# Causal attention on one core: value products of two steps issued in one run

## The reference

```python
Q = (X @ Wq.T + bq).reshape(B, S, H, d_head) * scale
K = (X @ Wk.T + bk).reshape(B, S, H, d_head) * scale
V = (X @ Wv.T + bv).reshape(B, S, H, d_head)
scores = jnp.einsum('bqhd,bkhd->bhqk', Q, K)
causal = jnp.tril(jnp.ones((S, S), bool))
scores = jnp.where(causal[None, None], scores, -jnp.inf)
attn = jax.nn.softmax(scores.astype(jnp.float32), axis=-1).astype(X.dtype)
out = jnp.einsum('bhqk,bkhd->bqhd', attn, V).reshape(B, S, D)
return out @ Wo.T + bo
```

## Time and profile before

| | |
|---|---|
| median of 3 runs | 2092.39 us (2077.45 to 2098.33) |
| profiled execution, span | 2086.8 us |
| TensorE busy | 1742.4 us (83%) |
| VectorE busy | 1398.7 us (67%) |
| ScalarE busy | 966.8 us (46%) |
| scores L1817, 768 | 304.2 us busy |
| units L1796, 768 | 254.2 us busy |
| values L1829, 1536 | 162.7 us busy |
| exponentials L1780, 768 | 346.4 us busy |
| row maxima L1697, 608 | 372.1 us busy |

### The profile page before, as it was taken

The page is one execution under the profiler, slowest core; times in us unless marked ns, Lnnn a source line. Parts: engine busy times, 40 slices in busy tenths (PEclk is TensorE's granted clock), DMA queues, the critical chain, the costliest instruction groups (busy, mean ns, idle before and its releaser), DMA issues. The chain is left out here.

```text
span 2086.8 us, 35358 instructions
## 1 busy us (share of the span) xinstructions
PE 1742.4 (83%) x10488; PEld 1335.8 (64%) x10488; DVE 1398.7 (67%) x2854; ACT 966.8 (46%) x2226; POOL 677.7 (32%) x845
## 2 busy tenths in 40 slices
PE   6998897189964664999999899996899999758886
PEld 5887785179963452554554454444699999647775
DVE  5567998056657865999777676643666776436666
ACT  2454564044435650565655555564434444323333
POOL 2444588300017612112146456520000000355540
PEclk8678999599986986999999999999999999879998
DMA  9213356344435874424245344315844444534441
GB/s 344 72 46 76 92 136 173 126 143 125 125 109 169 283 264 93 97 56 94 63 117 143 101 136 137 105 53 150 245 153 126 125 124 127 164 89 137 145 130 34
DMA packets 291880, 272.78 MB, mean 131 GB/s; under 512 B 138153, under 2 KB 260714, under 8 KB 289644
## 3 DMA queue, kind: packets, MB, share of 16 engines
q1 hardware_dynamic: 267960, 215.41, 35.6%
q0 software_dynamic: 18432, 50.36, 7.8%
q10 hardware_dynamic: 5332, 4.96, 0.7%
HBM read 136.84 MB, written 133.69 MB: 130 GB/s over the span
## 5 line engine op out<-in xcount | busy, mean ns | idle before, releaser
L1780 ACT ACTIVATE ca_PT<-ca_psS 128x512 f32<-128x512 f32 (+3 forms) x768 | 346.4, 492 | 285.5 <-PE ca_psS L1817 243.3
L1697 DVE TENSOR_REDUCE ca_part<-ca_psM 128x1 f32<-128x512 f32 (+3 forms) x608 | 372.1, 657 | 137.9 <-PE ca_psM L1800 104.6
L1817 PE MATMUL ca_psS<-ca_QS,ca_KS 128*128 128x512 f32 (+3 forms) x768 | 304.2, 403 | 12.3 <-ACT ca_PT L1780 12.1
L1796 PE MATMUL ca_psM<-ca_KS,ca_QS 126*128 126x512 f32 (+3 forms) x768 | 254.2, 376 | 55.2 <-DMA ca_KS<-ca_one_rows 39.5
L1072 POOL DMA_INDIRECT g_y<-ys_scratch,pos x128 | 130.3, 1018 | 477.0 <-POOLq L68 385.1
L1817 PEld LDWEIGHTS ca_psS<-ca_QS,ca_KS 128*128 128x128 f32 x768 | 147.5, 194 | 147.9 <-ACT ca_PT L1780 93.0
L1796 PEld LDWEIGHTS ca_psM<-ca_KS,ca_QS 126*128 126x128 f32 x768 | 142.4, 197 | 86.7 <-issue 42.3
L1829 PE MATMUL ca_psO<-ca_PT,ca_VA 128*17 128x512 f32 (+3 forms) x1536 | 162.7, 496 | 10.2 <-DVE ca_OT L1723 9.0
L950 PE MATMUL f_psU<-ffn_hi,f_x_hi 128*128 x428 | 156.4, 365 | 0.0
L762 PE MATMUL fa_psO<-fa_weighed,ident 128*128 128x256 f32 x512 | 133.0, 419 | 26.3 <-DVE fa_weighed L555 26.3
L1674 POOL TENSOR_TENSOR ca_waited<-ca_waited 1x1 f32<-1x1 f32 x128 | 25.5, 200 | 364.7 <-ACT ca_PT L1780 363.7
(11 more groups left out here) (254 smaller groups left out, 4382.8 us busy)
## 6 DMA issues: line engine op xcount, KB each, us to landing
xs_scratch<-fa_blank SPq DMA_DIRECT2D x32, 640.0 KB
x_sb<-xs_scratch SPq DMA_DIRECT2D x143, 128.0 KB, 2.1
ys_scratch<-x_sb SPq DMA_DIRECT2D x143, 128.0 KB, 1.7
ca_QS<-qk_scratch SPq DMA_DIRECT2D x32, 512.0 KB
ca_KS<-qk_scratch SPq DMA_DIRECT2D x32, 512.0 KB
xs_scratch<-fa_blank SPq DMA_DIRECT2D x32, 384.0 KB, 5.8
x_sb<-in_ffn SPq DMA_DIRECT2D x16, 608.0 KB, 4.1
room<-xs_scratch SPq DMA_DIRECT2D x71, 128.0 KB, 2.1
```

The lines of the kernel that those rows point to most:

```text
L1697: dve.tensor_reduce(dst, psM[(n * NU + u) % BANKS][:, 0:nh * w].rearrange("p (h k) -> p h k", h=nh), AX.X, ALU.max)\
L1780: act.activation(PT[:, s % PTS, h, off:CHUNK], psS[(GH * s + h) % BANKS][:, off:CHUNK], ACT.Exp)\
L1796: ins = pe.matmul(bank[:, h * w:(h + 1) * w], QS[0:STACK, slot, h0 + h, qt * P:(qt + 1) * P], KS[0:STACK, slot, h0 + h, k0:k0 + w], start= ...
L1817: pe.matmul(psS[tile % BANKS][:, off:CHUNK], KS[:, slot, h, kt * P:(kt + 1) * P], QS[:, slot, h, c * CHUNK + off:(c + 1) * CHUNK], start=T ...
```

## The change

Value steps are issued two at a time, only at odd steps: behind the scores and units of step s come value steps s - 3 and s - 2. `LAG` becomes 3 and `PTS` 4, so there is a fourth buffer of exponentials, and ScalarE starts step s when value step s - 4 is done. The end of the last round is fitted to it.

```diff
-    SLOTS, PTS, LAG = 3, 3, 2
+    SLOTS, PTS, LAG = 3, 4, 3
...
-                if n * NS + s >= LAG:
-                    values(*divmod(n * NS + s - LAG, NS))
+                if n * NS + s >= LAG and (n * NS + s) % 2:
+                    for m in range(n * NS + s - LAG, n * NS + s - LAG + 2):
+                        values(*divmod(m, NS))
...
-            for s in range(NS - LAG, NS):
+            for s in range(NS - LAG + 1, NS):
                 values(ROUNDS - 1, s)
```

## The result

The changed kernel takes 2134.49 us (median of 4, 2124.41 to 2142.47), the kernel before 2091.21 in the same comparison (2077.45 to 2098.33): a ratio of 1.0212, interval 1.0179 to 1.0245. The forecast was 2113; the time lies above the range.

A forecast was written before the change was run, and what follows sets the result against it. Attention rounds were taken as bound by TensorE's order of work, with VectorE nearly the bound in rounds 0 to 3. Terms -0.4 + 10.9 + 4.8 + 4.4 + 1.7 = +21 us, median about 2113, range 2084 to 2131.

The forecast's parts named there:

- rounds 4 and 5: Attention rounds 4 and 5: each gains the 0.2 us of a plain round, -0.4 us in all.
- rounds 0 to 3: Routing rounds, VectorE nearly the bound: it starves 1.2 us at each of four long value runs a round, +10.9 us.
- rounds 6 to 13, order and hold-up: Burst rounds: the value step free inside the hold-up now comes behind it; +0.6 us a round, +4.8 in all.
- rounds 6 to 13, clock: Burst rounds: two more falls of TensorE's clock to 1.2 GHz, 2.2 us each, +4.4; upper bound six more, +13.
- rounds 14 and 15: Round 14's second half and 15, ScalarE the bound: one longer idle per pair, +0.3 us for some six pairs, +1.7.
- the price of the burst in rounds 6 to 13: Rounds with nine GpSimd transfers in a row: order and hold-up +4.8 us plus clock +4.4.
- the rival that the clock falls in every burst: Rounds 6 to 13: six more clock falls instead of two, +30 us in all, 2122 us; chance 0.15.
- Plain rounds: Round 5: steps 10 and 11 lose 0.8 us, 2 and 3 gain 0, four other pairs gain 1.0: 0.2 gained.
- the saving of the switches: TensorE in the attention: 0.3 us saved per switch to value steps, 95 fewer switches, 28.5 us less work.
- The two rules: Skill rules: same-row weight loads would show, 10 us less saved; banks in turn with small idles make the clock alternate.

The follow-up runs named there:

- experiment 6: Changed kernel with value steps alone at steps 2 to 5, other pairs and the burst of nine kept: 2120.0 us in one run (2087.62 before).
- Experiment 5: Changed kernel with value step 4 alone again at step 6 and value step 5 at step 7, burst of nine kept: 2123.4 us, 1.0191.
- experiment 1: Changed kernel with VectorE's row maxima taken over only the first half of each unit's columns: 2064.93 us, ratio 0.9863 to the kernel before.
- 7 and 8: Five transfers in a row instead of nine, the rest two behind each later cut: kernel before 2091.32 us, changed kernel 2102.22 us, one run each.
- experiments 10 and 11: VectorE's copy, division and routing put behind its reductions, burst spread: changed kernel (pairs) 2058.1 us, 0.9884; kernel before (single steps) 2124.67 us, 1.019.
- experiment 4: Changed kernel with GpSimd's transfers spread as two behind each cut, not nine in a row: 2086.55 us, ratio 0.9977 to the kernel before.

## Why the prediction was wrong

| term | forecast | measured |
|---|---|---|
| rounds 4 and 5 | -0.4 | +0.6 |
| rounds 0 to 3 | +10.9 | +15.3 |
| rounds 6 to 13, order and hold-up | +4.8 | about +14 (estimate) |
| rounds 6 to 13, clock | +4.4 | about +13 (estimate) |
| rounds 14 and 15 | +1.7 | +0.1 |
| sum | +21 | +43.3 |

- **The step that failed: the price of the burst in rounds 6 to 13, +9.2 for 27.3 measured, in both of its terms.** The two were not run apart, so the split is an estimate from busy and idle time.
- **"Two more falls: +4.4."** It was six more, one in each of the eight rounds. A fall shows mostly as busy time: round 8 before was 2.84 us longer than round 6 and 2.79 busier, round 10 of experiment 6 2.81 longer than round 11 and 2.50 busier. Busy time rose by 10.2 us in rounds 6 to 13, and the pair order by itself takes 8 x 0.36 = 2.9 off it (33.44 before, 33.08 changed, in round 5). So the six falls cost some 13 us, 2.2 each: the price that the forecast gave a fall, and the upper bound of its term. The number of falls was wrong. This is the rival that the clock falls in every burst. I held six rounds at 1.00 against it; experiment 6, where seven of eight rounds had a fall without more idle, shows that they were no sign of safety. Nor would that rival's own time have been enough: 2122.
- **"Order and hold-up: +4.8."** The other 14 us lie above its upper bound of 9.6. The plain order is 8 x 0.23 = 1.8 of them; 12.4 is TensorE standing idle in the hold-up (17.1, less 8 x 0.59 for the plain order: 1.26 us idle in round 5 against 0.67), 1.5 us a round. The forecast left the hold-up as deep as it was and charged only the value step that no longer fills it, 0.88 - 0.3 a round. Experiment 5 puts that step back, and the idle falls by 6.1 us only. Round 11 of experiment 1 says the same at full clock: 4.7 us for 3.6. Where single steps stand in front of the burst (experiment 6) it is hardly deeper, and with five in a row (7 and 8) not at all. Why pairs in front of nine transfers make it deeper is open.
- **Rounds 0 to 3.** Rounds 0 and 2, at full clock, lost 2.81 and 2.90 us: four such are 11.4, the forecast's 10.9. Rounds 1 and 3 lost 4.58 and 5.00, and in both the clock fell after a wait for VectorE, of 1.36 and 1.84 us. Step 3 of round 1, changed kernel:

```profile
881.61 0.44 PE L1796 MATMUL ca_psM<-ca_KS,ca_QS 126*128 126x384 f32 x1 [1.36 <-DVE ca_part L1697]
...
883.23 3.18 PE L1829 MATMUL ca_psO<-ca_PT,ca_VA 128*17 128x512 f32 x16
886.35 0.65 PE L1817 MATMUL ca_psS<-ca_QS,ca_KS 128*128 128x512 f32 x1
```

  The run of values takes 3.1 us here, nearly twice the 1.63 of round 5's steps 2 and 3 (1037.67 to 1039.30). That the clock is the whole of the extra 4 us was not tried by itself.
- **Plain rounds: right to half a microsecond**, a loss of 0.23 (round 5) for a gain of 0.2. Steps 10 and 11 took 6.34 for 6.4, steps 2 and 3 took 5.85 (1033.45 to 1039.30) for the 5.74 of before, taken as no change. The other four gain 0.6 together, not 1.0. Experiment 1 shows the saving of the switches when nothing takes it back (0.22 each, not 0.3), experiments 10 and 11 that VectorE's other work in front of its reductions was most of what took it.
- **The last two rounds** lost nothing; ScalarE's second idle was not worth what I gave it.
- **The two rules.** On weight loads (the Trainium skill, TensorE: Matmul & The Clock Gate, The mechanism) the rows decide as forecast: two steps of 512 columns in a run take 1.84 us, and 0.66 / 384 us a column makes 1.76 of them, so the second step's loads add nothing that shows. On banks taken in turn (the Trainium skill, TensorE: Matmul & The Clock Gate, the second failure mode) the answer is in two parts. In rounds 6 to 13 of experiment 4 TensorE takes the same banks in turn at a clock of 1.00, so turns with small idles alone do not do it. In rounds 1 and 3 the fall follows a wait for such a bank, of 1.36 us in round 1; there the trace agrees. But another wait of 1.36 us, in round 3 (before the unit at 959.56), was followed by no fall.

## What to carry to other kernels

Work that is taken in longer runs on the engine that sets the time is worth its saved switches only if the engine that hands back its buffers keeps its own pauses elsewhere: put that engine's odd jobs behind the run, in the same edit. A stage that already shows a fall of the clock in some of its rounds must be taken as one where another order may bring the fall in all of them, even one that adds no idle (experiment 6), and be priced so. And look first at what makes the hold-up: spreading nine transfers was worth 31.6 us of the attention, the new order of the values and of VectorE's work 7.

## What the hardware showed that was not expected

While GpSimd issues indirect transfers in a row, 1.27 us apart, ScalarE and VectorE start up to 3.5 us late on matmuls that are long done. It begins some five microseconds into the burst (burst from 1072.96, first late score 1078.14) and is still there a microsecond after its last transfer (1084.08; the score of 1083.74 is read at 1085.17). Five in a row cost 1.6 us a round in either order, nine 3.45 to 4.7 at full clock, two behind each cut nothing with single steps and 0.8 with pairs. That the transfers are the cause is shown by spreading them; what in them holds the updates up is not settled.
